# Feed-forward products as plain fp32 matmuls of 32 columns, in one pipeline over 256 steps

## What is computed

```python
x = x + tanh(g_xattn) * attention(layernorm(x), ctx)      # 16 heads, 77 context rows
h = layernorm(x) @ W1 + b1                                # 512 -> 2048
i = w_imag * sin(theta + 0.1 * h)
q = h + (cos(theta) * w_real + sin(theta) * w_imag) * i * 0.1
x = x + tanh(g_ffn) * (relu(q) @ W2 + b2)                 # 2048 -> 512
```

## Time and profile before

| | us |
|---|---|
| median of 3 runs (lowest, highest) | 2136.9 (2136.64, 2137.37) |
| the profiled execution | 2137.62 |
| its span, first to last instruction | 2135.8 |
| attention stage, from the span's start | 734.2 |
| feed-forward stage | 1401.6 |

### The profile page before, as it was taken

One profiled execution on the slowest core, in us unless ns is written; L12 is line 12 of the kernel. 1 busy time (PEld: TensorE's weight loads), 2 busy tenths in 40 slices (PEclk: granted clock), 3 DMA queues, 4 the chain that ended last, 5 costly groups with the idle time before them and its releaser, 6 DMA issues.

```text
span 2135.8 us, 29046 instructions
## 1 busy us (share of the span) xinstructions
PE 2112.7 (99%) x10331; PEld 1709.8 (80%) x10331; DVE 1436.0 (67%) x2457; ACT 1163.2 (54%) x3463; POOL 398.5 (19%) x324
## 2 busy tenths in 40 slices
PE   9999999999999999999999999999999999999999
PEld 7777777777777778888888888888888888888887
DVE  5587778778776587666665666656666666566654
ACT  3487777777777465444444444444454444544443
POOL 3043443344443311010110100101101011010110
PEclk9999999999999999999999999999999999999999
DMA  7644444454453351231222312213123122231210
GB/s 237 153 115 117 128 114 121 124 117 116 127 120 98 130 137 60 60 79 60 40 72 47 79 60 60 66 42 70 60 60 79 60 40 66 53 79 59 40 40 21
DMA packets 372491, 181.88 MB, mean 85 GB/s; under 512 B 294390, under 2 KB 308954, under 8 KB 372346
## 3 DMA queue, kind: packets, MB, share of 16 engines
q1 hardware_dynamic: 371274, 179.52, 33.1%
q0 software_dynamic: 640, 0.47, 0.1%
q10 hardware_dynamic: 432, 0.04, 0.0%
HBM read 106.34 MB, written 56.85 MB: 76 GB/s over the span
## 4 chain that ended last, share of the span: by engine, by line
PE 64%; DVE 1%; ACT 0%; issue 0%; ACTq 0%; DVEq 0%
PE pair_bank L56 32%; PE m_bank L56 32%; DVE w_split L1474 0%; DVE hidden L1508 0%; DVE turns L1504 0%; DVE sine L1501 0%; ACT relu L1434 0%; ACT hidden L1443 0%; ACT turns L1445 0%; DVE stats L181 0%; DVE relu L1491 0%; DVE x_in L206 0%; ACT sine L1450 0%; DVE residual L1516 0%; DVE mean L191 0%
## 5 line engine op out<-in xcount | busy, mean ns | idle before, releaser
L56 PE MATMUL pair_bank<-w_split,relu 128*128 128x512 f32 x3072 | 738.3, 389 | 3.9 <-DVE relu L1491 3.2
L56 PE MATMUL m_bank<-xT,w_split 128*128 128x512 f32 x3024 | 726.3, 389 | 0.0
L56 PEld LDWEIGHTS pair_bank<-w_split,relu 128*128 128x128 f32 x3072 | 576.1, 188 | 125.4 <-issue 3.6
L56 PEld LDWEIGHTS m_bank<-xT,w_split 128*128 128x128 f32 x3024 | 567.6, 188 | 117.9
L1450 ACT ACTIVATE sine<-turns 128x512 f32<-128x512 f32 x256 | 161.8, 632 | 393.5 <-DVE turns L1504 393.5
L947 ACT ACTIVATE exps<-pair_bank,lowest 128x77 f32<-128x77 f32 x1024 | 316.7, 348 | 62.7 <-DVE lowest L1116 62.5
L1434 ACT ACTIVATE relu<-hidden 128x512 fp32r<-128x512 f32 x256 | 161.9, 632 | 331.4 <-PE m_bank L56 232.1
L1491 DVE SCALAR_TENSOR_TENSOR relu<-hidden,relu 128x512 fp32r<-128x512 f32 x256 | 181.2, 708 | 202.4 <-ACT relu L1434 202.4
L1508 DVE SCALAR_TENSOR_TENSOR hidden<-sine,sine_gain,hidden 128x512 f32<-128x512 f32 x256 | 197.0, 769 | 169.9 <-ACT sine L1450 169.9
L201 POOL TENSOR_TENSOR rstd<-var_eps,minus_half 128x4 f32<-128x4 f32 x32 | 38.2, 1194 | 1156.7 <-DVE var_eps L197 1156.7
L947 ACT ACTIVATION_READ_ACCUMULATOR exps<-pair_bank,lowest 128x1 f32 x1024 | 235.1, 230 | 0.0
(11 more groups left out here) (136 smaller groups left out, 1711.9 us busy)
## 6 DMA issues: line engine op xcount, KB each, us to landing
residual<-in_x_dram SPq DMA_DIRECT2D x64, 256.0 KB, 2.7
x_scratch<-residual SPq DMA_DIRECT2D x64, 256.0 KB, 2.1
x_in<-x_scratch SPq DMA_DIRECT2D x16, 1024.0 KB, 5.6
residual<-x_scratch SPq DMA_DIRECT2D x64, 256.0 KB, 3.3
out_dram<-residual SPq DMA_DIRECT2D x64, 256.0 KB, 2.1
quad_scratch<-x_in SPq DMA_DIRECT2D x60, 256.0 KB, 4.8
x_in<-quad_scratch SPq DMA_DIRECT2D x60, 256.0 KB, 4.4
x_in<-in_x_dram SPq DMA_DIRECT2D x8, 1024.0 KB, 6.5
```

The source lines that it names most:

```text
L56: mm = pe.matmul(out, stationary(s), moving(m), start=first and n == 0, stop=last and n == len(PASSES) - 1)
```

## The change

The split is dropped in the feed-forward block. Weights, x and relu stay plain fp32. Each 128-column matmul becomes four of 32 columns, each writing its own strip of 32 partitions of the bank: 16 matmuls a product in place of 12. Weight chunks are loaded to their final place (`w1_rest`, `w2_rest`, and `w_chunk` for the first three) with a semaphore each, so nothing waits for a split. The low-part work (DVE), the high-part copies of weights (ACT) and POOL's copy of the early chunks go; the x of the next batch is copied once (`turned`, ACT). In `front`, the last batch's split of x and the early weight splits go.

The stage becomes one loop over 256 steps: first products run three steps ahead and use four banks (`m_bank` and the two `t_bank`); `hidden` has four buffers, `turns`, `sine` and `relu` three. In one iteration n ACT reads bank n twice, takes the sine of step n-1 and the relu of step n-2; DVE rounds step n and mixes step n-1. The gated outputs of a batch are taken at step 2 of the next one, around that step's rounding. `x_turn` moves to f = 11 and 12, the copies to f = 12 and 13. On SP eight chunk loads are issued at once at the start of the stage, and `regroup_x(1)` comes before the last five.

```diff
         def ffn(st):
-            AHEAD = 2
+            AHEAD, KEPT = 3, 3
+            TOTAL = FT * B
             LN_AT, NORM_AT = 2, 4
-            TURN_AT = {9: (0, 1), 10: (2, 3)}
-            XT_AT = {9: (0, 1), 10: (2, 3)}
-            w1_split = [sb(st, f"w1_split{i}", [P, KT, F], F32R) for i in range(2)]
-            w2_split = [sb(st, f"w2_split{i}", [P, FT, D], F32R) for i in range(2)]
+            TURN_AT = {11: (0, 1), 12: (2, 3)}
+            XT_AT = {12: (0, 1), 13: (2, 3)}
+            w1_rest = sb(st, "w1_rest", [P, FT // HT - 2, CHUNK])
+            w2_rest = sb(st, "w2_rest", [P, FT // HT - 1, CHUNK])
+            xf = [sb(st, f"xf{s}", [P, KT, N]) for s in range(2)]
...
-            hidden = [sb(st, f"hidden{i}", [P, N]) for i in range(2)]
-            turns = sb(st, "turns", [P, N])
-            sine = sb(st, "sine", [P, N])
-            relu = [[sb(st, f"relu{s}_{i}", [P, N], F32R) for i in range(2)] for s in range(2)]
+            hidden = [sb(st, f"hidden{i}", [P, N]) for i in range(KEPT + 1)]
+            relu = [sb(st, f"relu{i}", [P, N]) for i in range(KEPT)]
+            turns = [sb(st, f"turns{i}", [P, N]) for i in range(KEPT)]
+            sine = [sb(st, f"sine{i}", [P, N]) for i in range(KEPT)]
+            h_bank = [*m_bank, *t_bank]
...
+                load_w1(2)
+                load_w2(1)
                 sp.dma_start(b2_rows[:, :], b2.rearrange("(a d) -> a d", a=1).to_broadcast([P, D])).then_inc(b2_loaded, 16)
+                for g in range(3, 6):
+                    load_w1(g)
+                    load_w2(g - 1)
                 for tile in range(NT):
                     sp.wait_ge(x1_stored[tile], 16 * B)
                     load_residual(0, tile)
-                for n in range(STAGED, CHUNKS):
-                    if n == NORM_AT + 2 * STAGED:
-                        regroup_x(1)
-                    sp.wait_ge(chunk_split, n - STAGED + 1)
-                    load_chunk(sp, n)
+                regroup_x(1)
+                for g in range(6, FT // HT):
+                    load_w1(g)
+                    load_w2(g - 1)
+                load_w2(FT // HT - 1)
                 load_x(2)
                 outputs(0, False)
...
-                def batch(b, slot, last):
-                    if not last:
+                pool.wait_ge(b2_loaded, 16)
+                pool.tensor_scalar(b2_rows[:, :], b2_rows[:, :], tanh_g[:, 1:2], 0.0, ALU.mult, ALU.add)\
+                    .then_inc(b2_gated, 1)
+                pool.wait_ge(b2_gated, 1)
+                for b in range(B):
+                    if b < B - 1:
                         rstd_of(pool, B + b + 2)
                     for tile in range(NT):
                         pool.wait_ge(residual_loaded[tile], 16 * (b + 1))
                         pool.tensor_tensor(residual[tile][:, :], residual[tile][:, :], b2_rows[:, :], ALU.add)\
                             .then_inc(residual_ready, 1)
...
-                pool.wait_ge(early_split, EARLY)
-                for i in range(2):
-                    pool.tensor_copy(w1_split[i][:, :, 0:EARLY * HT * P], xT[1][i][:, :, :].bitcast(F32)).then_inc(early_kept, 1)
-                pool.wait_ge(b2_loaded, 16)
...
+                def first_product(n):
+                    b, f = divmod(n, FT)
+                    if b == 0 and f % HT == 0:
+                        g = f // HT
+                        if g < 2:
+                            pe.wait_ge(chunk_loaded[g], 16)
+                        else:
+                            pe.wait_ge(w1_loaded[g], 16)
+                    if b and f == 0:
+                        pe.wait_ge(x_ready, KT * b)
+                    if n >= len(h_bank):
+                        pe.wait_ge(h_ready, n - len(h_bank) + 1)
+                    bank = h_bank[n % len(h_bank)]
                     for kt in range(KT):
-                        early = b == 0 and f < EARLY * HT
-                        mm = matmul3(pe, tiles_of(m_bank[f % 2][:, :]),
-                                     lambda p: (xT[1] if early else w1_split)[p][:, kt, f * P:(f + 1) * P],
-                                     lambda p: by_tiles(xT[slot][p], kt) if b == 0 else tiles_of(xT[slot][p][:, kt, :]),
-                                     kt == 0, kt == KT - 1)
+                        for j in range(HG):
+                            strip = slice(j * DH, (j + 1) * DH)
+                            mm = pe.matmul(tiles_of(bank[:, :])[strip], w1_chunk(f // HT)[:, kt, f % HT * P + j * DH:f % HT * P + (j + 1) * DH],
+                                           by_tiles(xT[0][1], kt).bitcast(F32) if b == 0 else tiles_of(xf[b % 2][:, kt, :]),
+                                           start=kt == 0, stop=kt == KT - 1)
...
+                def second_product(n):
+                    b, f = divmod(n, FT)
+                    if b == 0 and f % HT == 0:
...
+                    pe.wait_ge(relu_ready, n + 1)
                     for tile in range(NT):
-                        if f == 0:
-
-                            pe.wait_ge(y_ready, NT * b + tile + 1)
-                        mm = matmul3(pe, pair_bank[tile // 2][:, tile % 2, :],
-                                     lambda p: relu[f % 2][p][:, tile * P:(tile + 1) * P],
-                                     lambda p: w2_split[p][:, f, :], f == 0, f == FT - 1)
+                        if f == 0 and b:
+                            pe.wait_ge(y_ready, NT * (b - 1) + tile + 1)
+                        for j in range(HG):
+                            strip = slice(j * DH, (j + 1) * DH)
+                            mm = pe.matmul(pair_bank[tile // 2][strip, tile % 2, :], relu[n % KEPT][:, tile * P + j * DH:tile * P + (j + 1) * DH],
+                                           w2_chunk(f // HT)[:, f % HT, :], start=f == 0, stop=f == FT - 1)
                         if f == FT - 1:
                             mm.then_inc(y_full, 1)
                     if f < FT - 1:
                         mm.then_inc(relu_used, 1)
...
+                for n in range(AHEAD):
+                    first_product(n)
+                for n in range(TOTAL):
+                    if n + AHEAD < TOTAL:
+                        first_product(n + AHEAD)
+                    second_product(n)
...
+                def turned(b, kts):
+                    act.wait_ge(blocks_turned, QUADS * b)
                     for kt in kts:
...
+                        act.activation(quad_order(xf[b % 2][:, kt, :]), x_quads[:, :, :, kt, :], ACT.Copy).then_inc(x_ready, 1)
...
+                def relu_of(n):
+                    act.wait_ge(mixed, n + 1)
...
+                    act.activation(relu[n % KEPT][:, :], hidden[n % (KEPT + 1)][:, :], ACT.Relu).then_inc(relu_ready, 1)
+                for n in range(TOTAL + 2):
+                    b, f = divmod(n, FT)
+                    if n < TOTAL:
+                        act.wait_ge(h_full, n + 1)
+                        if n > KEPT:
+                            act.wait_ge(relu_ready, n - KEPT)
+                        act.activation(hidden[n % (KEPT + 1)][:, :], h_bank[n % len(h_bank)][:, :], ACT.Identity,
+                                       bias=b1_col[:, f:f + 1])
+                        act.activation(turns[n % KEPT][:, :], h_bank[n % len(h_bank)][:, :], ACT.Identity, scale=0.1 / TWO_PI,
+                                       bias=turns_phase[:, f:f + 1]).then_inc(h_ready, 1)
+                    if 1 <= n <= TOTAL:
+                        act.wait_ge(part_ready, n)
+                        act.activation(sine[(n - 1) % KEPT][:, :], turns[(n - 1) % KEPT][:, :], ACT.Sin, scale=TWO_PI_BELOW)\
+                           .then_inc(sine_ready, 1)
+                    if n >= 2:
+                        relu_of(n - 2)
+                    if b < B - 1 and f in XT_AT:
+                        turned(b + 1, XT_AT[f])
...
+                def whole_turns(n):
+                    dve.wait_ge(h_ready, n + 1)
+                    if n >= KEPT:
+                        dve.wait_ge(mixed, n - KEPT + 1)
+                    dve.tensor_scalar(sine[n % KEPT][:, :], turns[n % KEPT][:, :], ROUND_MAGIC, ROUND_MAGIC, ALU.add, ALU.subtract)\
                        .then_inc(whole_ready, 1)
...
+                def mix(n):
+                    dve.wait_ge(sine_ready, n + 1)
...
+                def outputs(b, tiles):
...
+                for n in range(TOTAL + 1):
+                    b, f = divmod(n, FT)
+                    done = b - 1 if b and n < TOTAL and f == AHEAD - 1 else None
+                    if done is not None:
+                        outputs(done, range(HALF))
+                    if n < TOTAL:
+                        whole_turns(n)
+                    if done is not None:
+                        outputs(done, range(HALF, NT))
+                    if n:
+                        mix(n - 1)
+                    if b < B - 1:
+                        if f == LN_AT:
+                            sums(dve, B + b + 2, x_in)
```

(52 more changed lines are left out.)

178 lines of the change are left out of this document (39 added, 139 removed).

## The result

The changed kernel takes 2497.4 us (median; 2496.45 to 2498.28) against 2137.1 (2136.64 to 2139.48) for the kernel before, run beside it: 1.168 times as long, 95% interval 1.1663 to 1.1703. That is 360 us slower, where 454 us faster was forecast, and outside the range given. The time is that of the rival "Slower", 2496, at which I had put 4 chances in 100.

What follows compares the result with a forecast made beforehand. PE's feed-forward matmuls bound the kernel. Stage start 734.2 + products 876.5 + start 2.1 + place A 42 + place B 22.5 + end 0.7 + tail 3.4 and 0.2 = 1681.6, adjusted to 1683 us; range 1618 to 1760.

Steps and rivals of the forecast that it cites:

- Slower: Rival, feed-forward stage: long runs of narrow fp32 strips get the lower clock level, 0.856 us a group, 2496 us; chance 0.04.
- The main term: PE's 512 feed-forward products: four groups at 0.428 us, 1.712 us each against 2.72; 876.5 us against 1392.6, 516 less.
- strips run one after another: Case in the feed-forward products: the four strips don't run side by side; slower still than 2496 us, excluded, no chance given.
- PE never waits: Rival, feed-forward stage: neighbouring operations overlap enough to swallow the stalls at Place A and Place B; 1618 us, chance 0.12.
- A product drains before the next: Rival, PE's feed-forward products: none runs into the next across their waits, 1.924 us each; 1762 us, chance 0.05.
- DVE and POOL bound each batch's head: Rival, batch start: DVE loses all four POOL adds, plus late residuals or x; 8 to 11 us a batch, 1738 to 1783, chance 0.09.
- Start: Start of the feed-forward stage: PE idles 2.1 us until the first relu; a slow clock afterwards (3 us) taken as 0.
- Place A: Step 2 of a batch: DVE's outputs, statistics and POOL's b2 adds delay relu; 3 us of stall, 14 batches, 42 us.
- the low end: Lower bound at step 2 of a batch: DVE's own operations in order delay relu, stalling PE 1.3 us.
- Place B: Steps 12 and 13 of a batch: ACT's x copies wait for DVE's transposes; 1.5 us of stall, 15 batches, 22.5 us.
- Weights and the order on SP: Feed-forward chunk loads, five behind batch 1's regrouping: PE waits taken as 0, at most 5 us; eight earlier, at most 8.
- ACT and DVE fit: Feed-forward step: ACT's 2.61 us and DVE's 2.00 fit in PE's 3.42, so PE remains the bound on average.

Runs made afterwards that it cites:

- one pass a group: Changed kernel with one full-width reduced-precision matmul in place of each four strips, weights, x and relu rounded, low parts left out: 1578.1 us.

## Why the prediction was wrong

**The main term.** "Four of them take 0.64 us from first start to last end, 24 take 2.78, so each further group of four adds (2.78 - 0.64) / 5 = 0.428 us." This step failed. The durations were right, the count was not: 24 records are 12 matmuls, so each further group of four matmuls adds twice that. The main term is 2048 x 0.859 = 1759.2 us instead of 876.5; with the start of the stage at 734.2 and the 3.6 us at its end that is 2497.0, and the span is 2496.4 us. Nothing is left for the other terms to explain. The code would have told it: three steps of four strips are 12 matmuls a head pair, not 24, while the split products of the same trace have as many records as matmuls (512 x 12 = 6144). The "16384" matmuls of the prediction are the same slip: the code has 8192.

**The doubt that was put aside.** The Trainium skill, FP8 and Floating Point Precision (TensorE Precision Notes), gives true fp32 four passes through the array. By that rule four passes replaced three; the runs agree with the price, 0.859 us against 2.72 / 12 = 0.227 for a reduced matmul, 3.8 times, while the passes themselves are not to be seen in a trace, which has two records. I had set "about two passes' time" against the rule and let the row decide; but the row's divisor, the number of matmuls, was assumed and not read. At the measured prices the change had to lose: 4 x 0.859 = 3.44 us a product against 12 x 0.227 = 2.72.

**The rivals.** "Slower" had the place and the price (0.856 a group, decided from 0.68) and the time, 2496. Its mechanism, the lower clock level, is not what happened: the granted clock is 1.00 in the whole stage. That the time came out is luck: anything that doubles the price of a group gives it. Half the pace in one form at full clock was in front of me as two passes against four, and I gave it no chance of its own. That strips run one after another was excluded by the first row, rightly: in the run with one strip of four, one costs as much as four (2494.95 us). "PE never waits" came true in the changed kernel, for a reason that is none of its own: a step of 6.87 us leaves ACT and DVE more slack than before. "A product drains before the next" is not seen: products start 3.43 to 3.44 us apart, before the last record of 3.64 ends. "DVE and POOL bound each batch's head" had the right engine, as the adds show, but not its price, 8 to 11 us a batch: with eight matmuls a product it is some 2.

**The smaller terms**, which the long products hide, show with eight reduced matmuls a product. Start: 2.1 forecast, 1.96 measured; the slow clock behind it, taken as 0, cost some 1.5 us in one run and nothing in the other. Place A: 3 us a batch between 0.8 and 5 forecast, 31 us over the batches or about 2 measured, nearly all of it from POOL's adds; DVE's own burst, the 1.3 us of the low end, didn't show at that step, which is 0.2 us longer than the one of the forecast. Place B: 1.5 forecast, 0.54 and 0.55 in the batches shown; over 15 batches that is some 8 us where the sum had 22.5. A part of the difference may lie in a reading: ACT's 2.61 us a step is the sum of four records, which overlap. In the changed kernel the four take 2.30 us from first start to last end (1298.32 to 1300.62), so ACT had more slack than the 0.8 us of the forecast. ACT's wait for the transposes is there in the changed kernel too, 30.9 us over 15 batches, 2.1 each, as the forecast's order of instructions had it (free at 2.6, transposes done at 4.4), but costs nothing. Weights and the order on SP: neither the changed kernel nor the one with eight matmuls shows a wait of PE for a chunk, so 0, as taken. "ACT and DVE fit" held.

## What to carry to other kernels

Before a duration from a trace prices an instruction, count that instruction in the code and its records in the trace: here a plain fp32 matmul leaves two, a reduced one leaves one, and the missing factor was the sign of the whole forecast. Three reduced-precision matmuls (0.68 us) are cheaper than one plain fp32 matmul (0.859 us) of the same shape, so where PE is the bound, giving up a split into high and low parts for plain fp32 loses. And when a row and a stated rule differ by a clean factor of two, the count in the row is the first thing to doubt.

## What the runs showed of the hardware that I had not expected

A plain fp32 matmul that moves 512 columns costs 0.859 us at granted clock 1.00, with 32 columns of weights or 128, alone or four strips side by side; its records last 592 ns each and come every 0.43 us. Beside POOL's adds of 128x512 (6.50 us for four, 1.6 each) DVE's operations take 1.5 to 1.8 us in place of 0.4 to 0.75, each about as long as one add. The Trainium skill, SBUF — State Buffer (Who interferes with whom), has the two engines share a pair of ports as an exclusive lock; the rows agree. Shortening the adds gave 31 us where PE was the bound, taking them away 64 where it was not. With one pass a group, PE waits for relu in 116 to 144 of the 256 steps and the granted clock of the stage is 0.88 to 0.90; every kernel whose PE was nearly always busy had 1.00.
